# Dense products of the relational passes: h in a 12-bit part and the rest, two float32r products per block in place of one float32

## The chip, the cores and the metric

The kernel runs on one core of a Trainium2 chip, in one launch. The metric is the device time of one execution in microseconds; the executions of the kernel before took 5861.25 to 5871.9 us, with a median of 5869.68. The engines are named as in the profile: PE (matmul), PEld (its weight loads), DVE (vector), ACT (scalar), POOL (gathers), SP (most of the other DMAs).

## The reference

A graph network over 3125 nodes of 256 numbers and 100000 edges with a source, a target and one of 4 relations. The targets are the same in all layers; the shapes are fixed, the edges are data.

```python
# first pass: one graph convolution with a residual and a layernorm
h = x @ W                                     # (3125,256)@(256,256)
norm = deg_inv_sqrt[src] * deg_inv_sqrt[dst]
out = segment_sum(h[src] * norm[:, None], dst)
x = layernorm(x + out)
# four relational layers
inv_deg = 1 / max(cnt[dst, etype], 1)
for l in range(4):
    h = einsum('ni,rio->rno', X, W[l])        # 4 products (3125,256)@(256,256)
    agg = segment_sum(h[etype, src] * inv_deg[:, None], dst)
    out = agg + X @ root[l] + bias[l]
    X = elu(layernorm(out) * gamma[l] + beta[l]) + X
out = layernorm(x + X)
```

## The kernel before

The nodes are cut into `NW` = 25 windows of 128. All work is done in five **passes** (q = 0 for the first convolution, 1 to 4 for the relational layers). A pass takes h, which the pass before has stored in DRAM (`h_table`), and adds up for each window of targets what its edges bring. The edges are counted and sorted once, before pass 0. They come in two kinds.

**Gathered edges.** They are sorted by target window and cut into `NT` = 588 tiles of 128 edges. For a tile POOL gathers 128 rows of h (L584, an indirect DMA) into one of `RING` = 20 slots (16 in `msg`, 4 in `hout`); DVE makes the one-hot matrix `emat` of its targets and weights, 8 tiles ahead (L1409; ACT does it in pass 0); PE multiplies them (L758, float32, two instructions of 256 columns each) into one of `NPS` = 4 PSUM banks; DVE adds the bank to the window's sum (L1429). A slot and a bank are free again when PE and DVE say so.

**Dense edges.** The `K` = 7 chunks (128 source nodes each) with the most edges are kept in SBUF for a whole pass: SP loads them at the start of a pass, 7 pieces of 512 KB (L467). Their edges, `NDE` = 28000, were counted before pass 0 into blocks of 128 x 128 counts, one per source chunk, target window and relation. Each window of each pass multiplies its 28 blocks with the cached rows of h (`dense_product`, L736, float32), 700 products in a pass, and DVE adds the four sums with their weights (L1571). SP fetches the blocks of the next window as soon as PE has used those of the present one (L512, 7 pieces of 256 KB).

**Order of the work.** On PE the products of the tiles stand in a fixed order, and everything else is put before a tile by a table (`put(work, tile, step)`): window j ends at tile `done_at[j]`, and its dense products and its own window work are set by these two rules (DVE's table `steps` is of the same kind):

```python
done_at = [(j + 1) * NT // NW for j in range(NW)]
def dense_tile(j, i):
    d = done_at[j - 1] if j else 0
    return d + 1 + i * 16 // (K * R) if j else 14 + i * 7 // (K * R)
```

The window work is the transposes of the new X (L682), the four products with the next layer's weights (L690, 512 columns) and with its root (L700, L703), then DVE's layernorm and elu, ACT's copies, and the storing of h (SP, L503). The next pass begins when all h is stored. PE waits for a tile's gather (`s_msg`), its one-hot (`s_em`), a free bank (`s_acc`), and ahead of a dense product for the cached chunks (`s_hc`), the counts (`s_counts`) and the sums of the window before (`s_dense`).

**Before pass 0** (the first 1400 us) DVE counts the edges of every source chunk, chooses the 7 (L1124 to L1138), and the edges are sorted into tiles; then the count blocks are built from `DT` = 318 tiles of dense edges (L807, L811, L840) and stored in DRAM.

## Time and profile before

| | |
|---|---|
| median of 3 executions | 5869.68 us |
| span of the profiled execution | 5905.4 us |
| PE busy | 4806.4 us, 81% |
| PE weight loads | 3355.2 us, 57% |
| DVE busy | 3711.0 us, 63% |
| POOL busy | 3267.9 us, 55% |
| ACT busy | 1418.0 us, 24% |
| before pass 0 | 0 to 1400 us |
| pass 0, 1, 2, 3, 4 begin at | 1405, 2296, 3201, 4103, 5004 us |

The profiled execution's own time is its span, 5905.4 us; it is 35.7 us longer than the median. The busy shares are means over stages that differ: the stages before pass 0 have little POOL work, and in the passes PE, DVE and POOL pass each tile on. A long busy time says nothing by itself; the idle times before instructions, with the engine that ended them, say who waits.

### The profile page before, as it was taken

How to read it: one execution, taken by the hardware profiler on the slowest of the kernel's cores; microseconds unless marked ns; L12 is line 12 of the kernel's file. 1: busy time of each engine (PE TensorE's matmuls, PEld its weight loads, DVE VectorE, ACT ScalarE, POOL GpSimd, SP SyncE). 2: the span in 40 equal slices, each digit the busy share in tenths (PEclk: the TensorE clock that was granted, in tenths of full speed). 3: DMA queues.
4: the chain of work that ended last, by engine and by line, in shares of the span. 5: the costliest groups of instructions: out<-in, count | busy, mean ns of one | idle time of the engine just before them, and what ended most of it. 6: DMA issues, size and time to landing. Idle time of an engine off the chain costs nothing.

```text
span 5905.4 us, 80081 instructions
## 1 busy us (share of the span) xinstructions
PE 4806.4 (81%) x20415; PEld 3355.2 (57%) x20415; DVE 3711.0 (63%) x9969; ACT 1418.0 (24%) x3629; POOL 3267.9 (55%) x3256
## 2 busy tenths in 40 slices
PE   5878876777888887888887888887888888777776
PEld 4544432345666665666664666665666665556555
DVE  7998885565666664555554555555556555566665
ACT  1046653213555551111111111111111111011011
POOL 0058871003666664666664666665666664666664
PEclk8999998999999998999998999998999998888888
DMA  1000016312555555555555555555555555444444
GB/s 49 1 1 1 1 21 228 143 61 89 159 156 161 162 158 170 161 157 155 159 157 150 162 156 159 159 155 161 155 158 155 159 159 152 144 143 145 143 140 126
DMA packets 398886, 772.61 MB, mean 131 GB/s; under 512 B 77327, under 2 KB 166113, under 8 KB 398424
## 3 DMA queue, kind: packets, MB, share of 16 engines
q0 software_dynamic: 150720, 386.19, 24.2%
q1 hardware_dynamic: 246824, 380.53, 19.2%
q8 instruction: 162, 2.65, 0.2%
q10 hardware_dynamic: 1008, 1.84, 0.1%
q14 instruction: 172, 1.41, 0.1%
HBM read 652.04 MB, written 115.89 MB: 130 GB/s over the span
## 4 chain that ended last, share of the span: by engine, by line
PE 65%; issue 13%; DVE 12%; another core or an unknown queue 5%; ACT 2%; DVEq 2%; DMA 1%; ACTq 0%; SPq 0%
PE psum L736 24%; PE psum L758 23%; PE psum L690 5%; PE psum L807 3%; DVE arena L1429 3%; PE psum L840 2%; PE psum L793 2%; DVE arena L1571 2%; DVE arena L1303 2%; DVE arena L1290 2%; PE psum L700 1%; DVE arena L1238 1%; PE psum L622 1%; DVE emat L1409 1%
## 5 line engine op out<-in xcount | busy, mean ns | idle before, releaser
L584 POOL DMA_INDIRECT msg<-h_table,g_rel x1880 | 1795.6, 955 | 1088.5 <-issue 419.9
L1429 DVE TENSOR_TENSOR arena<-arena,psum 128x256 f32 x2940 | 1224.7, 417 | 1434.8 <-PE psum L758 970.4
L758 PE MATMUL psum<-msg,emat 128*128 128x256 f32 x4704 | 1519.7, 413 | 547.7 <-issue 323.1
L758 PEld LDWEIGHTS psum<-msg,emat 128*128 128x128 f32 x4704 | 892.9, 202 | 1021.7 <-issue 795.6
L1409 DVE TENSOR_SCALAR emat<-iota,node,weight 128x128 f32<-128x128 f32 x2352 | 862.9, 368 | 139.4 <-issue 58.8
L736 PE MATMUL psum<-arena,emat 128*128 128x256 f32 x3200 | 908.1, 405 | 6.3 <-issue 6.1
L584 POOL DMA_INDIRECT msg<-h_table,g_src x472 | 457.0, 968 | 726.3 <-PE psum L758 591.0
L736 PEld LDWEIGHTS psum<-arena,emat 128*128 128x128 f32 x3200 | 647.5, 204 | 134.0 <-issue 35.5
L566 POOL DMA_INDIRECT placed_rows<-leaving,idx x300 | 439.6, 1465 | 423.3 <-issue 416.7
L584 POOL DMA_INDIRECT hout<-h_table,g_rel x472 | 451.3, 956 | 275.4 <-issue 110.2
L793 PE MATMUL psum<-arena,emat 125*128 125x453 f16 x2000 | 448.0, 358 | 85.9 <-DVE arena L1303 85.9
L1376 DVE SCALAR_TENSOR_TENSOR found<-iota,key,arena 128x512 f16<-128x512 f32 x588 | 440.6, 749 | 87.3 <-issue 35.5
L758 PE MATMUL psum<-hout,emat 128*128 128x256 f32 x1176 | 377.9, 411 | 141.5 <-issue 82.5
L690 PE MATMUL psum<-w_sb,xt 128*128 128x512 f32 x800 | 445.8, 647 | 18.4 <-issue 16.3
L736 PE MATMUL psum<-arena,more_blocks 128*128 128x256 f32 x1600 | 425.6, 379 | 0.0
L758 PEld LDWEIGHTS psum<-hout,emat 128*128 128x128 f32 x1176 | 220.7, 200 | 259.4 <-issue 210.7
L1028 ACT ACTIVATE emat<-emat,arena 125x128 f16<-125x128 f16 x1000 | 302.9, 387 | 214.1 <-DVE emat L1282 214.1
L736 PEld LDWEIGHTS psum<-arena,more_blocks 128*128 128x128 f32 x1600 | 304.9, 191 | 41.8
L793 PEld LDWEIGHTS psum<-arena,emat 125*128 125x128 f16 x2000 | 163.4, 98 | 261.0 <-DVE arena L1303 145.7
L999 ACT ACTIVATE emat<-hout,ones 128x128 f32<-128x128 f32 x588 | 210.2, 395 | 392.0 <-PE psum L758 296.0
L736 PE MATMUL psum<-hout,more_blocks 128*128 128x256 f32 x1000 | 277.1, 381 | 0.0
L909 ACT COPY hout<-psum 128x512 f32<-128x512 f32 x200 | 114.0, 582 | 645.1 <-remote 314.1
(253 smaller groups left out, 5331.1 us busy)
## 6 DMA issues: line engine op xcount, KB each, us to landing
emat<-count_blocks SPq DMA_DIRECT2D x496, 256.0 KB
more_blocks<-count_blocks SPq DMA_DIRECT2D x372, 256.0 KB
count_blocks<-emat SPq DMA_DIRECT2D x200, 256.0 KB
h_table<-hout SPq DMA_DIRECT2D x100, 512.0 KB
msg<-h_table,g_rel POOLq DMA_INDIRECT x1880
arena<-h_table SPq DMA_DIRECT2D x24, 512.0 KB
msg<-h_table,g_src POOLq DMA_INDIRECT x472
hout<-h_table,g_rel POOLq DMA_INDIRECT x472
```

Source lines behind the costliest of these rows:

```text
L566: pool.indirect_dma_start(out=placed_dram[:, :], out_offset=bass.IndirectOffsetOnAxis(ap=idx[0:EP, n:n + 1], axis=0), in_=leaving[:, n, :] ...
L584: pool.indirect_dma_start(out=slots[n % RING], out_offset=None, in_=table[:, :], in_offset=bass.IndirectOffsetOnAxis(ap=rows[:, t:t + 1], ...
L690: mm = pe.matmul(win_ps[h][:, :], xt[:, 0, k * P:(k + 1) * P], w_sb[:, k, 2 * h:2 * h + 2, :].rearrange("p r o -> p (r o)"), start=(k == 0 ...
L736: mm = pe.matmul(to, blocks[c][:, r * P:(r + 1) * P], rows, start=(c == 0 and first), stop=(c == K - 1 and last))
L758: pe.matmul(agg_ps[n % NPS][:, 0:D], emat[:, n % BODY, :], slots[n % RING], start=True, stop=True).then_inc(s_mm, 1)
L793: pe.matmul(ps[half][:, 0:HB], slot[:, n, :], tile_hot[:, n, half * HB:(half + 1) * HB], start=False, stop=False)
L807: return pe.matmul(cols(psum, at, R * P), zeros16[:, 0:P], zeros16[:, :], start=True, stop=False)
L999: act.activation(emat[:, t % BODY, :], square[:, i * P:(i + 1) * P], ACT.Relu, bias=ones[:, 0:1], scale=-1.0).then_inc(s_em, 1)
L1028: a = act.activation(slot[:, n, :], lane_hot[:, b, m, :], ACT.Copy, scale=val[:, bass.ds(i * SU + k, 1)])
L1376: return dve.scalar_tensor_tensor(found[:, :, :], key_v, key[:, t:t + 1], inv_v[:, :, bass.ds(w, 1), :].rearrange("p r w d -> p r (w d)"), ...
L1409: dve.tensor_scalar(emat[:, n % BODY, :], iota[:, 0:P], node[:, t:t + 1], weight[:, t:t + 1], ALU.is_equal, ALU.mult).then_inc(s_em, 1)
L1429: dve.tensor_tensor(a, a, agg_ps[n % NPS][:, 0:D], ALU.add).then_inc(s_acc, 1)
```

## The change

1. `dense_product`: in passes 1 to 4 each block is multiplied twice, as float32r, with the two parts of h in the new tile `cache` (K x R x 2 x 256 float32r). Pass 0 keeps its one float32 product.
2. The parts: SP loads a chunk into part 1; DVE masks off the low 12 bits into a scratch tile (`cache_mask`), ACT copies it as float32r into part 0 (`high_parts`), DVE subtracts part 0 from part 1 (`cache_rest`). These steps stand among DVE's steps 3 to 16 of each relational pass. PE waits for each chunk (`s_split`) in the first window.
3. A chunk takes at most `MOST` = 4096 edges. The choice of chunks is written anew with this cap. `NDE` goes from 28000 to 26321, `NT` from 588 to 600, `DT` from 318 to 304.
4. Slot and relation of a dense edge are put in its sort key, and its decoding is written for that.
5. SBUF: the new cache takes the place of what only the stages before pass 1 need; the blocks have a tile of their own (`counts`); the x of the last residual is no longer loaded whole at the start of pass 1, but 128 KB per window in the last pass (`fetch_x1`).

```diff
-    NDE = E * K // NW
+    MOST = 1 << 12
+    NDE = min(MOST * f + (K - f) * (E - MOST * f) // NW for f in range(K + 1))
...
+        cache = sb("cache", [P, K, R, 2, D], f32r)
...
+                        sp.dma_start(cache[:, i, :, 1, :].bitcast(f32),
+                                     h_views[q % 2][bass.ds(c, 1), :, :, :]
+                                     .rearrange("w p r o -> (w p) r o")).then_inc(s_hc[i], 16)
...
-                if q == 1:
-
+                if q == L:
                     sp.wait_ge(s_x1w, (NW + ONE0) * 16)
-                    sp.dma_start(X1.rearrange("p (w d) -> p w d", w=NW),
-                                 x1_dram.rearrange("(w p) d -> p w d", p=P)).then_inc(s_x1, 16)
 
                 def store(j):
...
+                def fetch_x1(j):
+                    v = window_at(mybir.EngineType.SP, j)
+                    if j >= 2:
+                        sp.wait_ge(s_fin, (j - 2) * NFIN + 2)
+                    sp.dma_start(x1_slots[j % 2], x1_view[bass.ds(v, 1), :, :]
+                                 .rearrange("w p d -> (w p) d")).then_inc(s_x1[j % 2], 16)
...
             def dense_product(q, j, i):
                 n, (c, r) = q * NW + j, divmod(i, R)
                 if i == 0:
-                    pe.wait_ge(s_hc, (q + 1) * (16 * K))
+                    if q == 0:
+                        pe.wait_ge(s_first_cache, 16 * K)
                     if n:
                         pe.wait_ge(s_dense, n)
                 if r == 0:
                     pe.wait_ge(s_counts[c], (n + 1) * 16)
+                    if q and j == 0:
+                        pe.wait_ge(s_split, (q - 1) * K + c + 1)
                 if q:
-                    to, first = dense_ps[r // 2][:, r % 2 * D:(r % 2 + 1) * D], r % 2 == 0
-                    last = r % 2 == 1
-                    rows = hcaches[c][:, r, :]
+                    for part in range(2):
+                        mm = pe.matmul(dense_ps[r // 2][:, r % 2 * D:(r % 2 + 1) * D],
+                                       blocks[c][:, r * P:(r + 1) * P], cache[:, c, r, part, :],
+                                       start=(c == 0 and r % 2 == 0 and part == 0),
+                                       stop=(c == K - 1 and r % 2 == 1 and part == 1))
                 else:
-                    to, first, rows = dense_ps[0][:, 0:D], r == 0, hcache0[c]
-                    last = r == R - 1
-                mm = pe.matmul(to, blocks[c][:, r * P:(r + 1) * P], rows,
-                               start=(c == 0 and first), stop=(c == K - 1 and last))
+                    mm = pe.matmul(dense_ps[0][:, 0:D], raw_blocks[c][:, r * P:(r + 1) * P],
+                                   hcache0[c], start=(c == 0 and r == 0),
+                                   stop=(c == K - 1 and r == R - 1))
                 if r == R - 1:
...
+            def high_parts(q):
+                for c in range(K):
+                    act.wait_ge(s_masked, (q - 1) * K + c + 1)
+                    act.copy(cache[:, c, :, 0, :], masked).then_inc(s_high, 1)
...
-            done(dve.scalar_tensor_tensor(size_key[:, :], misc_ps[:, 256:256 + NW], 32.0,
-                                          iota[:, 0:NW], ALU.mult, ALU.add))
-            done(dve.tensor_tensor(pair_a, over_windows(size_key[:, :]),
-                                   by_window(size_key[:, :]), ALU.is_gt))
-            done(dve.tensor_reduce(place[:, :], pair_a, AXX, ALU.add))
-            done(dve.tensor_tensor(pair_a, over_windows(place[:, :]), by_window(iota[:, 0:NW]),
-                                   ALU.is_equal))
-            done(dve.tensor_tensor(pair_b, pair_a, over_windows(iota[:, 0:NW]), ALU.mult))
-            done(dve.tensor_reduce(top[:, :], pair_b, AXX, ALU.add))
+            for i in range(K):
+                done(dve.scalar_tensor_tensor(place[:, :], taken[:, :], float(-MOST),
+                                              misc_ps[:, 256:256 + NW], ALU.mult, ALU.add))
+                done(dve.tensor_scalar(place[:, :], place[:, :], 0.0, float(MOST),
+                                       ALU.max, ALU.min))
+                done(dve.scalar_tensor_tensor(size_key[:, :], place[:, :], 32.0, iota[:, 0:NW],
+                                              ALU.mult, ALU.add))
+                done(dve.tensor_reduce(best[:, :], size_key[:, :], AXX, ALU.max))
+                dve.scalar_tensor_tensor(chosen[:, :], size_key[:, :], best[:, :], iota[:, 0:NW],
+                                         ALU.is_equal, ALU.mult, accum_out=top[:, K - 1 - i:K - i])
+                done(dve.scalar_tensor_tensor(order[:, :], size_key[:, :], best[:, :],
+                                              taken[:, :], ALU.is_equal, ALU.mult,
+                                              accum_out=part_of[:, K - 1 - i:K - i]))
+                done(dve.scalar_tensor_tensor(taken[:, :], size_key[:, :], best[:, :],
+                                              taken[:, :], ALU.is_equal, ALU.add))
             done(dve.tensor_copy(top_i[:, :], top[0:1, 0:K]))
+            for i in range(K):
+                done(dve.tensor_scalar(hits[2], s_hi, top[0:EP, i:i + 1], 0.0,
+                                       ALU.is_equal, ALU.add, accum_out=row_n[0:EP, i:i + 1]))
+            dve.sem_inc(s_tot, 1)
+            dve.wait_ge(s_base, 2)
+            dve.tensor_copy(row_first[0:EP, :], misc_ps[0:EP, 0:K])
+            done(dve.tensor_scalar(top_rank[0:EP, :], part_of[0:EP, :], float(MOST), float(MOST),
+                                   ALU.mult, ALU.add))
             for i in range(K):
                 done(dve.tensor_scalar(hits[2], s_hi, top[0:EP, i:i + 1], float(i + 1),
                                        ALU.is_equal, ALU.mult))
-                done(dve.tensor_tensor(d_place, d_place, hits[2], ALU.add))
+                done(dve.tensor_scalar(hits[1], hits[2], 1.0, None, ALU.min))
+                done(dve.tensor_tensor_scan(runs[2], one_row, hits[1], row_first[0:EP, i:i + 1],
+                                            ALU.mult, ALU.add))
+                done(dve.scalar_tensor_tensor(hits[2], runs[2], top_rank[0:EP, i:i + 1], hits[2],
+                                              ALU.is_le, ALU.mult))
+                done(dve.tensor_tensor(d_place, d_place, hits[2], ALU.max))
             done(dve.tensor_scalar(hits[2], d_place, 0.0, None, ALU.is_gt, ALU.add,
...
-            split_values(a_d, b_d, c_d, e_d)
+            done(dve.tensor_scalar(c_d, a_d, 2, P - 1, ALU.arith_shift_right, ALU.bitwise_and))
+            done(dve.tensor_scalar(e_d, b_d, 10, None, ALU.arith_shift_right))
+            dve.scalar_tensor_tensor(d_slot[:, :], e_d, float(P), c_d, ALU.mult, ALU.add)
+            done(dve.tensor_scalar(b_d, b_d, 3, P - 1, ALU.arith_shift_right, ALU.bitwise_and))
+            done(dve.tensor_scalar(a_d, a_d, R - 1, None, ALU.bitwise_and))
             done(dve.scalar_tensor_tensor(d_key[:, :], a_d, float(P), b_d, ALU.mult, ALU.add))
-            done(dve.tensor_scalar(e_d, c_d, P - 1, None, ALU.bitwise_and))
-            done(dve.tensor_copy(d_slot[:, :], e_d))
-            done(dve.tensor_scalar(c_d, c_d, 7, None, ALU.arith_shift_right))
-            chunk, part = e_d.bitcast(f32), a_d.bitcast(f32)
-            done(dve.tensor_copy(chunk, c_d))
-            for i in range(K):
-                if i % KH:
-                    done(dve.tensor_scalar(part, chunk, top[:, i:i + 1], float(i % KH * P),
-                                           ALU.is_equal, ALU.mult))
-                    done(dve.tensor_tensor(d_slot[:, :], d_slot[:, :], part, ALU.add))
...
+            def cache_mask(q, c):
+                dve.wait_ge(s_hc[c], q * 16)
+                dve.wait_ge(s_high, (q - 1) * K + c)
+                dve.tensor_scalar(masked.bitcast(i32), cache[:, c, :, 1, :].bitcast(i32),
+                                  HI_MASK, None, ALU.bitwise_and).then_inc(s_masked, 1)
+
+            def cache_rest(q, c):
+                dve.wait_ge(s_high, (q - 1) * K + c + 1)
+                dve.tensor_tensor(cache[:, c, :, 1, :], cache[:, c, :, 1, :].bitcast(f32),
+                                  cache[:, c, :, 0, :].bitcast(f32), ALU.subtract
+                                  ).then_inc(s_split, 1)
...
+                if q:
+                    for c in range(K):
+                        steps[SPLIT0 + c * SPLITS] = lambda c=c: cache_mask(q, c)
+                        steps[SPLIT0 + 1 + c * SPLITS] = lambda c=c: cache_rest(q, c)
+                assert SPLIT0 + K * SPLITS <= done_at[0] - DA
```

PE, the first dense products of pass 1 (window 0). A row's count is of matmul calls; a float32 call of 128x256 is two instructions in the trace. The program names a tile by its place in memory, so the cached rows and count blocks read as `hout` and `emat` before. Before:

```order
L758 MATMUL psum<-msg,emat 128x256 x14
L736 MATMUL psum<-hout,emat 128x256 x4
L758 MATMUL psum<-msg,emat 128x256
L736 MATMUL psum<-hout,emat 128x256 x4
L758 MATMUL psum<-msg,emat 128x256
L736 MATMUL psum<-hout,emat 128x256 x4
```

and now:

```order
L803 MATMUL psum<-msg,emat 128x256 x14
L775 MATMUL psum<-cache,counts 128x256 x8
L803 MATMUL psum<-msg,emat 128x256
L775 MATMUL psum<-cache,counts 128x256 x8
L803 MATMUL psum<-msg,emat 128x256
L775 MATMUL psum<-cache,counts 128x256 x8
```

The dense products stand ahead of the same tiles, and each call of float32 has become two of float32r.

PE again, the last dense products of a window in the same pass, where the next layer's products (L690, now L731) begin. Before:

```order
L682 MATMUL psum<-ident,hout 128x128 x2
L736 MATMUL psum<-w_sb,more_blocks 128x256 x2
L758 MATMUL psum<-msg,emat 128x256
L736 MATMUL psum<-w_sb,more_blocks 128x256
L758 MATMUL psum<-msg,emat 128x256
L736 MATMUL psum<-w_sb,more_blocks 128x256 x2
L758 MATMUL psum<-hout,emat 128x256
L736 MATMUL psum<-w_sb,more_blocks 128x256
L736 MATMUL psum<-hout,more_blocks 128x256
L758 MATMUL psum<-hout,emat 128x256
L690 MATMUL psum<-w_sb,xt 128x512
L736 MATMUL psum<-hout,more_blocks 128x256 x2
```

and now:

```order
L803 MATMUL psum<-hout,emat 128x256
L775 MATMUL psum<-cache,counts 128x256 x4
L803 MATMUL psum<-hout,emat 128x256
L723 MATMUL psum<-ident,hout 128x128 x2
L775 MATMUL psum<-cache,counts 128x256 x4
L803 MATMUL psum<-hout,emat 128x256
L775 MATMUL psum<-cache,counts 128x256 x2
L803 MATMUL psum<-msg,emat 128x256 x3
L731 MATMUL psum<-w_sb,xt 128x512
```

The spread over 16 tiles is as it was (two products ahead of most tiles, one ahead of some), with twice the calls; the layer products follow it a few tiles later.

DVE, the start of pass 1: one-hots (L1409, now L1479) and adds (L1429, now L1499; a row ISA is its wait). Before:

```order
L1409 TENSOR_SCALAR emat<-iota,node,weight 128x128 x8
L1416 TENSOR_LOAD win_i
L1409 TENSOR_SCALAR emat<-iota,node,weight 128x128
L1429 ISA
L1429 TENSOR_TENSOR arena<-arena,psum 128x256
L1409 TENSOR_SCALAR emat<-iota,node,weight 128x128
L1429 ISA
L1429 TENSOR_TENSOR arena<-arena,psum 128x256
L1409 TENSOR_SCALAR emat<-iota,node,weight 128x128
L1429 ISA
```

and now:

```order
L1499 ISA
L1499 TENSOR_TENSOR acc<-acc,psum 128x256
L1479 TENSOR_SCALAR emat<-iota,node,weight 128x128
L1499 ISA
L1499 TENSOR_TENSOR acc<-acc,psum 128x256
L1650 TENSOR_SCALAR hout<-cache 128x1024
L1479 TENSOR_SCALAR emat<-iota,node,weight 128x128
L1499 ISA
L1499 TENSOR_TENSOR acc<-acc,psum 128x256
L1655 TENSOR_TENSOR cache<-cache 128x4x256
L1479 TENSOR_SCALAR emat<-iota,node,weight 128x128
```

From the third add on, a mask (L1650) or a subtraction (L1655) stands between an add and the next one-hot, 14 of them in 14 steps.

## Rows read from the trace of the kernel before

**Rows 1.** Busy time by stage; columns: stretch, length, engines, clock, DMA share, GB/s.

```profile
0.00:330.00 330.00, 241.26 (x1217) 159.68 (x1217) 284.83 (x533) 19.03 (x51) 4.90 (x15) 0.92 0.08 22
...
900.00:1400.00 500.00, 359.99 (x1890) 183.08 (x1888) 280.83 (x980) 105.23 (x196) 18.67 (x20) 0.93 0.32 121
1400.00:2296.00 896.00, 764.68 (x2976) 562.14 (x2976) 568.63 (x1571) 450.00 (x1351) 552.12 (x568) 0.95 0.52 155
2296.00:3200.00 904.00, 764.36 (x2976) 566.21 (x2976) 510.05 (x1476) 138.40 (x225) 561.84 (x588) 0.95 0.53 160
...
4110.00:5004.00 894.00, 760.64 (x2974) 566.31 (x2974) 511.87 (x1475) 139.33 (x225) 555.96 (x583) 0.95 0.53 157
5004.00:5905.00 901.00, 681.18 (x2576) 518.50 (x2576) 537.62 (x1593) 89.30 (x125) 561.69 (x588) 0.87 0.49 143
```

**Rows 2.** The same for 100 us of pass 3 and of pass 4.

```profile
4300.00:4400.00 100.00, 85.48 (x349) 64.19 (x349) 58.10 (x169) 16.11 (x26) 64.72 (x69) 0.99 0.53 160
5200.00:5300.00 100.00, 79.52 (x310) 60.45 (x310) 62.23 (x190) 10.71 (x15) 65.39 (x69) 0.89 0.49 145
```

**Rows 3.** The page's part 4, the chain that ended last.

```profile
PE 65%; issue 13%; DVE 12%; another core or an unknown queue 5%; ACT 2%; DVEq 2%; DMA 1%; ACTq 0%; SPq 0%
PE psum L736 24%; PE psum L758 23%; PE psum L690 5%; PE psum L807 3%; DVE arena L1429 3%; PE psum L840 2%; PE psum L793 2%; DVE arena L1571 2%; DVE arena L1303 2%; DVE arena L1290 2%; PE psum L700 1%; DVE arena L1238 1%; PE psum L622 1%; DVE emat L1409 1%
```

**Rows 4.** Sums of waits: who waited for whom, us, times, longest.

```profile
POOL msg L584 <- PE psum L758: 978.4, 512, 481.9
DVE arena L1429 <- PE psum L758: 970.4, 618, 14.9
```

**Rows 5.** Timeline, PE, pass 4; columns: start, length, instruction, idle before.

```profile
5407.86 1.03 PE L736 MATMUL psum<-arena,emat 128*128 128x256 f32 x4
...
5412.61 1.03 PE L736 MATMUL psum<-arena,emat 128*128 128x256 f32 x4
5414.76 0.67 PE L758 MATMUL psum<-hout,emat 128*128 128x256 f32 x2 [1.12 <-issue]
```

**Rows 6.** Timeline, DVE, at the same place.

```profile
5414.19 0.42 DVE L1429 TENSOR_TENSOR arena<-arena,psum 128x256 f32 x1 [5.21 <-PE psum L758]
```

**Rows 7.** Timeline, POOL, in pass 1.

```profile
2601.05 0.94 POOL L584 DMA_INDIRECT hout<-h_table,g_rel  x1 [0.30 <-issue]
...
2606.65 0.94 POOL L584 DMA_INDIRECT hout<-h_table,g_rel  x1 [2.16 <-PE psum L758]
```

**Rows 8.** Timeline, PE, in pass 1.

```profile
3019.58 1.03 PE L736 MATMUL psum<-arena,emat 128*128 128x256 f32 x4
3020.44 0.59 PE L758 MATMUL psum<-msg,emat 128*128 128x256 f32 x2
```

**Rows 9.** Timeline, PE, while the count blocks are built (float16).

```profile
1100.00 0.60 PE L840 MATMUL psum<-emat 128*128 128x512 f16 x2
1100.43 0.17 PE L811 MATMUL psum<-zeros 128*128 128x1 f16 x1
```

**Rows 10.** The page's part 5: weight loads in float32 and in float16.

```profile
L736 PEld LDWEIGHTS psum<-arena,emat 128*128 128x128 f32 x3200 | 647.5, 204 | 134.0 <-issue 35.5
...
L793 PEld LDWEIGHTS psum<-arena,emat 125*128 125x128 f16 x2000 | 163.4, 98 | 261.0 <-DVE arena L1303 145.7
```

**Rows 11.** Timeline, DVE, choice of the chunks.

```profile
45.07 0.18 DVE L1124 SCALAR_TENSOR_TENSOR size_key<-psum,iota 128x25 f32<-128x25 f32 x1
...
49.70 0.43 DVE L1135 TENSOR_SCALAR arena<-arena,top 125x800 f16<-125x800 f16 x1
50.16 0.58 DVE L1137 TENSOR_TENSOR arena<-arena 125x800 f16<-125x800 f16 x1
...
57.22 0.99 DVE L1138 TENSOR_SCALAR_CACHE_REDUCE arena<-arena 125x800 f16<-125x800 f16 x1
...
60.99 1.88 DVE L1147 TENSOR_TENSOR_SCAN arena<-arena,d_first 125x800 f32<-125x800 f32 x1
```

**Rows 12.** Timeline, DVE, start of pass 1.

```profile
2322.19 0.42 DVE L1429 TENSOR_TENSOR arena<-arena,psum 128x256 f32 x1 [3.95 <-remote]
```

117 lines of the change are left out of this document (76 added, 41 removed).

## The prediction

> **What bounds the kernel now.** I read first the busy times by stage, to see whether the 81% of PE is an average over unlike stages. It is not quite. In each pass over the edges PE is busy 764 of about 904 us, DVE 510, POOL 562, and POOL issues 588 gathers, one per tile [rows 1]. Preparation before the first pass takes 1400 us. The last pass is the most telling row: it has 400 matmuls fewer, PE is busy 681 us instead of 761, and it still takes 901 us where the pass before took 894. The slices of 100 us say the same: 69 gathers in a slice of pass 3, with 85.5 us of PE, and 69 in a slice of pass 4, with 79.5 us of PE [rows 2]. That is a pace of 100 / 69 = 1.45 us per tile. A reader is to see here that PE time taken out of a pass need not come back as span.
>
> Then the chain of waits: 24% of the span runs through the dense product (L736), 23% through the tile product (L758), 12% through DVE and 13% is "issue", an engine waiting for nothing that shows [rows 3]. The sums of waits name the loop: DVE's add waits 970 us for the tile product, POOL's gather 978 us for the same line (a slot of the ring comes free when the tile is multiplied) [rows 4]. The timeline shows how. One stretch of PE, from 5407.86 on, is without a gap four rows of L758 (a tile each) and five of L736 with 18 instructions in all; the four tiles fill the four PSUM banks; DVE's first add comes only at 5414.19, after 5.21 us of idling, and PE starts again at 5414.76 after 1.12 us idle [rows 5, 6]. So a round of the loop is the stream of four tiles plus about 1.1 us.
>
> The third limit is POOL. A gather is 0.94 us and the next follows after 0.30, that is one per 1.25 us; a stall on the ring costs 2.16 instead of 0.30 [rows 7]. 1.25 us is the floor of a tile whatever PE does.
>
> **The dense products (the main term).** One block now costs two instructions of float32, started 0.216 us apart: 3019.58 to 3020.44 is four of them, 0.86 us [rows 8]. So a block is 0.433 us, and 700 of them in a pass are 303 us. After the change a block is also two instructions, each one float32r product of 256 columns. The trace has no float32r. The nearest row with a 2-byte type is the float16 product of 512 columns: two of them are passed in 0.43 us (1100.00 to 1100.43), 0.216 each, so 0.108 for 256 columns [rows 9]. Bounds: below, 0.108 an instruction, 0.216 a block; above, float32r as float32, two instructions of 0.216 for each of the two products, 0.866 a block. Between them stands the weight load: 204 ns mean for these float32 blocks, 98 ns for float16 [rows 10]; each block's weights are loaded twice, as now. At 0.2 us a load a block would cost 0.4 and nothing is won. I take 0.108 an instruction because both instructions and weights of one pass are near it in the float16 rows. That takes 0.217 x 700 = 152 us of PE work from each of passes 1 to 4, 608 in all; pass 0 keeps float32.
> The Trainium skill bears on this from both sides. "FP8 and Floating Point Precision", section TensorE Precision Notes, has true float32 as four passes and a reduced float32 that is read and cut to about 22 bits; a block in two single passes would be half of four, as the sum has it. "TensorE: Matmul & The Clock Gate", section on weight-path modes, gives the fast weight load to 128 weights of a type that is not FP32; if float32r counts as FP32 there, the weights stay at the 0.2 of the row, and the sum loses its main term. That is the fourth case below.
>
> **What of it reaches the end.** The order puts the dense products between tiles, 16 tiles of a window of 23.5; on average 28 x 2 / 16 = 3.5 instructions a tile. A round of four such tiles is (8 + 14) x 0.216 + 1.1 = 5.85 us, 1.46 a tile, which is the measured pace. After: 8 x 0.216 + 14 x 0.108 + 1.1 = 4.34 us, 1.09 a tile, below the 1.25 of POOL. So in these stretches the gather becomes the bound, but not cleanly: the ring is full, the sign of "done" comes in clumps of four, and each clump that comes late makes one gap of 2 us in POOL. The 7.5 tiles of a window without dense work keep their transposes and layer products. I take the mean of the present pace and the floor, weighted to the floor: 1.33 us per tile. Over the some 560 tiles of a pass that run at the pace now, that is 560 x 0.13 = -73 us a pass.
>
> **The tiles.** At most 4096 edges of a cached chunk become counts, which makes the dense part smaller: 26321 edges instead of 28000. NT goes from 588 to 600, so 12 gathers, products, one-hots and adds more in each of five passes. In passes 1 to 4, 12 x 1.33 = +16; in pass 0, 12 x 1.46 = +17.5. The building of the count blocks has 304 tiles instead of 318; that stage is at most 500 / 318 = 1.57 us a tile [rows 1]; 14 x 1.3 = -18.
>
> **The splitting.** In each pass from 1 on DVE masks and subtracts 7 chunks of 128x1024 and ACT copies them. DVE has nothing like it; the scan of 800 columns and the 800-column operation of 0.99 us [rows 11] bracket it at 0.7 to 1.3 us each, so about 13.5 us of DVE per pass and 7 of ACT. At the start of a pass DVE waits some 4 us before each add (3.95 before the one at 2322.19) [rows 12], and the split's steps, 3 to 16, lie just there; the order below the diff shows mask and subtraction between the adds. PE needs chunk c at tile 14 + c. The cover is these waits; without it the price is 13.5 us, and with a copy that DVE waits for, 20. Bounds 0 and +20 a pass; I take +5. DVE's in-order queue is the risk: the mask waits for a load of 512 KB, and the adds and one-hots behind it wait too.
>
> **Preparation.** The choice of the chunks is seven rounds of seven small operations at about 0.2 each (one over 25 columns took 0.18), 10 us, for the six operations that now stand from 45.07 to 49.5; seven counts at 0.99 and the reading of the sum, 8 us; and per chunk five operations of 800 columns with a scan of 1.88 instead of two (0.43 and 0.58 [rows 11]): 4.5 instead of 1.1, 24 us. With three more operations some +41; the shorter decoding gives 4.5 back. DVE is on the path there (285 of 330 us busy). Bounds +15 and +45. Net of preparation: 41 - 4.5 - 18 = +18.5.
>
> **Hidden edits.** x1 is no longer loaded as one 3.2 MB piece at the start of pass 1 but 128 KB a window in the last pass; DMA is at 0.53 and 0.49 of its time [rows 1], so I cost it at 0, with -8 to +10 as bounds. Loads of the cache are waited for one by one: 0, since the weights and blocks come as late.
>
> **Sum.** Passes 1 to 4: (-73 + 16 + 5) x 4 = -208. Pass 0: +17.5. Preparation: +18.5. Together -172 us on a span of 5905.4, so 5733. The median of the runs is 5869.7, 35.7 below that execution; the same distance gives 5698, say 5700. About 12 us (0.2%) is what a measurement here can tell from no change.
>
> **Rivals.**
> 1. Forecast: pace 1.33. For it: the round worked out above gives the pace now. Against: pass 4. 5700; its own range 5600 to 5810. Chance 0.39.
> 2. The floor: every tile at 1.25, as POOL's rows between stalls. 560 x 0.21 = -118, + 15 + 5, x 4 = -392, and +36: 5514. For it: 1.09 is well below 1.25. Against: POOL stalls at present though PE has gaps. Chance 0.21.
> 3. The other side: the pace stays 1.46. Pass 4 lost 80 us of PE work and gained nothing, so the loop PE - DVE - POOL may have its own period (DVE sees the four products late, POOL sees its slots late). Part of it can be the clock: it was granted 0.87 in pass 4 against 0.95 before [rows 1], and a less busy PE would again lose in clock what it gains in work. Then the price decides: 12 x 1.46 x 5 = 88, split 20, preparation 18.5: +126, 5996. It decides once the pace stays above 1.42. Chance 0.33. The skill's clock page ("TensorE: Matmul & The Clock Gate", HAM oscillation) has the same effect: PE that micro-idles between groups is throttled again and again; the 0.87 agrees in direction.
> 4. The change doesn't do what it says: float32r instructions are bound by 0.2 us weight loads (then as 3, about 6000) or run as float32, 0.433 more a block, x 2800 = +1212, about 7200. For it: the weight row of 204 ns. Chance 0.07, most of it at 6000.
>
> **From these the numbers.** Faster: 0.39 + 0.21, and a little of 3 where the pace falls to 1.40: 0.62. Same: between 1.40 and 1.42, 0.03. Slower: 0.35. The range 5490 to 6010 leaves out a floor that is undercut and float32r as float32. Since both signs have weight, the likeliest's own range stands above.
>
> **What the next profile would show.** Right: L775 at about 0.11 us between starts, with weight loads near 0.1; passes 1 to 3 near 850 us with 600 gathers, 73 to 75 gathers in a slice of 100 us; "POOL msg <- PE" much smaller. DVE's mask and subtraction within the first 60 us of a pass and no new wait before them; first stage longer by 40 us. Wrong if: weight loads of 0.2 set L775's starts (4), or 68 to 69 gathers a slice with PE more idle and a clock below 0.9 (3), or 79 to 80 gathers a slice (2).

## The result, and the profile after

The changed kernel took 5979.48 us (median of 4 runs, 5971.05 to 5985.01) against 5867.16 before on the same chip: ratio 1.0193, 95% interval 1.018 to 1.0205, 112 us slower. The profiled execution has a span of 5969.3 us.

Chips differ. The kernel before takes 5867 to 5913 us on some and 5235 to 5237 on two others (below: chips of the slower and of the faster kind), so every comparison of times here is between kernels on one chip. The profile of before that the prediction read has a span of 5905.4 us and is like the chip on which before took 5912.55 us in later runs; the profile below is from a chip on which gathers come 1.457 us apart in pass 1 instead of 1.475.

Busy time by stage of the changed kernel (columns as in [rows 1]): count blocks, pass 0, pass 1, pass 3 and pass 4.

```profile
940.00:1434.00 494.00, 351.16 (x1821) 178.22 (x1822) 273.74 (x953) 111.77 (x217) 19.52 (x21) 0.92 0.35 130
1434.00:2338.00 904.00, 763.07 (x2996) 566.44 (x2995) 586.35 (x1606) 454.98 (x1359) 559.51 (x580) 0.95 0.51 154
2338.00:3248.00 910.00, 698.05 (x3000) 523.76 (x3000) 532.09 (x1514) 145.42 (x231) 575.64 (x600) 0.87 0.52 157
...
4157.00:5065.00 908.00, 693.81 (x3000) 516.33 (x3000) 531.94 (x1515) 147.12 (x232) 577.46 (x600) 0.89 0.53 158
5065.00:5969.00 904.00, 612.25 (x2600) 487.62 (x2600) 556.91 (x1630) 97.91 (x133) 577.32 (x600) 0.78 0.50 148
```

Each pass takes 904 to 910 us, somewhat more than the 894 to 904 of [rows 1], though PE is busy some 66 us less (698 and 764 in pass 1), and 69 us less in pass 4. The granted clock went from 0.95 to 0.87 and 0.89 in passes 1 and 3, and from 0.87 to 0.78 in pass 4. Slices of 100 us, against [rows 2]:

```profile
4300.00:4400.00 100.00, 78.21 (x347) 58.13 (x346) 58.66 (x169) 15.30 (x26) 65.83 (x69) 0.91 0.51 156
5200.00:5300.00 100.00, 70.81 (x291) 56.71 (x292) 64.44 (x193) 9.14 (x13) 66.27 (x70) 0.74 0.50 149
```

69 gathers there before, 69 now; 69 in the last pass before, 70 now, with 70.8 us of PE instead of 79.5. The page's chain of waits, against [rows 3]: the dense product has gone from 24% to 16% (L775 with 11% in passes 1 to 4, L780 with 5% in pass 0), and "issue" (13% to 16%) and the tile product (L803, 23% to 26%) have taken its place.

```profile
PE 61%; issue 16%; DVE 13%; another core or an unknown queue 3%; ACT 2%; DVEq 2%; DMA 1%; SPq 0%; POOL 0%; ACTq 0%
PE psum L803 26%; PE psum L775 11%; PE psum L731 5%; PE psum L780 5%; DVE acc L1499 4%; PE psum L838 3%; PE psum L852 3%; PE psum L885 2%; DVE acc L1641 2%; DVE arena L1379 2%; DVE arena L1366 2%; PE psum L741 1%; DVE emat L1479 1%; PE psum L656 1%
```

The sums of waits, against [rows 4]: POOL and DVE still wait for the product of the tile.

```profile
POOL msg L618 <- PE psum L803: 846.1, 434, 468.7
DVE acc L1499 <- PE psum L803: 781.4, 554, 14.4
```

How one tile's product is passed on is seen on PE (start, length, instruction, idle before), with DVE and POOL below. The sign of a product is the semaphore update by which PE tells DVE and POOL that it is done.

```profile
3002.76 0.82 PE L775 MATMUL psum<-cache,counts 128*128 128x256 f32 x4
3003.43 0.67 PE L803 MATMUL psum<-msg,emat 128*128 128x256 f32 x2
...
3004.41 0.67 PE L803 MATMUL psum<-msg,emat 128*128 128x256 f32 x2
...
3010.46 0.67 PE L803 MATMUL psum<-msg,emat 128*128 128x256 f32 x2 [2.42 <-issue]
```

```profile
3009.89 0.42 DVE L1499 TENSOR_TENSOR acc<-acc,psum 128x256 f32 x1 [2.56 <-remote]
```

```profile
3503.79 0.94 POOL L618 DMA_INDIRECT hout<-h_table,g_rel  x1 [0.30 <-issue]
3505.04 0.95 POOL L618 DMA_INDIRECT hout<-h_table,g_rel  x1 [0.30 <-issue]
3507.75 0.94 POOL L618 DMA_INDIRECT hout<-h_table,g_rel  x1 [1.76 <-remote]
```

Three things are to be seen. The tile product that starts at 3004.41 ends in the record at 3005.08; DVE adds it at 3009.89, 4.8 us later, and had been idle for 2.56 us before. PE, with all four banks full, starts again at 3010.46 after 2.42 us idle, more than the 1.12 of [rows 5]. POOL keeps its 1.25 us between stalls of 1.76 where it waits for a slot.

The four float32r instructions from 3002.76 to 3003.43 seem to take 0.67 us, against 0.86 for four of float32 [rows 8], but this reading misleads: the first of them starts in the record too soon after the float32 product ahead of it. From one tile product to the next is the safe measure. In the run with half the gathers (below), where PE hardly waits, it is 0.90 us with two blocks between:

```profile
3200.39 0.59 PE L805 MATMUL psum<-msg,emat 128*128 128x256 f32 x2
3200.63 0.82 PE L777 MATMUL psum<-cache,counts 128*128 128x256 f32 x4
3201.28 0.60 PE L805 MATMUL psum<-msg,emat 128*128 128x256 f32 x2
```

The median of 427 such stretches in passes 1 and 2 is 0.900 us, and 1.295 (of 436) in its partner with float32 products; with one block between it is 0.671 and 0.863. So the second block adds 0.23 us in float32r and 0.43 in float32: an instruction of float32r takes 0.115 us, whether the weights change before it or not.

The weight load of a block did not get shorter as the float16 one is:

```profile
L775 PE MATMUL psum<-cache,counts 128*128 128x256 f32 x5600 | 1355.3, 363 | 41.6 <-issue 41.4
L775 PEld LDWEIGHTS psum<-cache,counts 128*128 128x128 f32 x5600 | 1002.4, 215 | 182.6 <-issue 75.9
```

Its mean record is 215 ns, while the products with these weights start 0.115 us apart: the loads overlap, and their length does not set the pace.

The split, at the start of pass 1 (mask, copy on ACT, subtraction, next mask):

```profile
2349.17 0.69 DVE L1650 TENSOR_SCALAR hout<-cache 128x1024 int32<-128x1024 int32 x1
...
2350.97 1.27 DVE L1655 TENSOR_TENSOR cache<-cache 128x1024 fp32r<-128x1024 f32 x1 [0.53 <-issue]
...
2352.75 0.68 DVE L1650 TENSOR_SCALAR hout<-cache 128x1024 int32<-128x1024 int32 x1
```

```profile
2349.89 1.05 ACT L997 CAST cache<-hout 128x1024 fp32r<-128x1024 f32 x1 [13.62 <-DVE hout L1650]
```

A chunk takes 3.6 us in the chain mask 0.69, copy 1.05, subtraction 1.27, between the adds. PE's idle time before L775 is 41.6 us in all four passes, 41.4 of it put down to "issue" and not to DVE. The choice of chunks (first small operation, first count, first scan, last STT of the seven):

```profile
44.75 0.18 DVE L1177 SCALAR_TENSOR_TENSOR place<-taken,psum 128x25 f32<-128x25 f32 x1
...
56.16 1.05 DVE L1193 TENSOR_SCALAR_CACHE_REDUCE arena<-arena,top 125x800 f16<-125x800 f16 x1
...
65.64 1.88 DVE L1204 TENSOR_TENSOR_SCAN arena<-arena,row_first 125x800 f32<-125x800 f32 x1
...
94.46 1.05 DVE L1206 SCALAR_TENSOR_TENSOR arena<-arena,top_rank 125x800 f16<-125x800 f32 x1
```

It ends at some 96.1 us; in the kernel before the last of these adds ended at 57.2 ([rows 11]). That is 39 us longer; 41 were forecast. POOL's first 20 gathers, which fill the ring long before pass 0, begin at 939.9 us instead of 899.8, 40 us later.

### The profile page after: what moved, and what is told of

Its sections match the earlier page's. It is cut to its first block, busy times and chain, and to the rows that moved or that the text cites. A ratio compares the mean times of both kernels' runs of the same rounds, so it can differ in the third digit from the quotient of the medians.

```text
span 5969.3 us, 80103 instructions
## 1 busy us (share of the span) xinstructions
PE 4519.0 (76%) x20453; PEld 3180.7 (53%) x20453; DVE 3830.7 (64%) x10216; ACT 1458.2 (24%) x3681; POOL 3334.8 (56%) x3316
## 3 DMA queue, kind: packets, MB, share of 16 engines
q14 instruction: 177, 1.45, 0.1%
## 4 chain that ended last, share of the span: by engine, by line
PE 61%; issue 16%; DVE 13%; another core or an unknown queue 3%; ACT 2%; DVEq 2%; DMA 1%; SPq 0%; POOL 0%; ACTq 0%
PE psum L803 26%; PE psum L775 11%; PE psum L731 5%; PE psum L780 5%; DVE acc L1499 4%; PE psum L838 3%; PE psum L852 3%; PE psum L885 2%; DVE acc L1641 2%; DVE arena L1379 2%; DVE arena L1366 2%; PE psum L741 1%; DVE emat L1479 1%; PE psum L656 1%
## 5 line engine op out<-in xcount | busy, mean ns | idle before, releaser
L803 PE MATMUL psum<-msg,emat 128*128 128x256 f32 x4800 | 1664.4, 442 | 742.8 <-issue 456.1
L1499 DVE TENSOR_TENSOR acc<-acc,psum 128x256 f32 x3000 | 1250.2, 417 | 1418.5 <-PE psum L803 781.4
L803 PEld LDWEIGHTS psum<-msg,emat 128*128 128x128 f32 x4800 | 893.1, 216 | 1166.4 <-issue 1003.5
L775 PE MATMUL psum<-cache,counts 128*128 128x256 f32 x5600 | 1355.3, 363 | 41.6 <-issue 41.4
L775 PEld LDWEIGHTS psum<-cache,counts 128*128 128x128 f32 x5600 | 1002.4, 215 | 182.6 <-issue 75.9
L1479 DVE TENSOR_SCALAR emat<-iota,node,weight 128x128 f32<-128x128 f32 x2400 | 876.6, 366 | 138.9 <-issue 80.6
L803 PE MATMUL psum<-hout,emat 128*128 128x256 f32 x1200 | 422.9, 443 | 194.2 <-issue 116.0
L838 PE MATMUL psum<-arena,build 125*128 125x452 f16 x2000 | 445.6, 356 | 87.6 <-DVE arena L1379 87.6
L731 PE MATMUL psum<-w_sb,xt 128*128 128x512 f32 x800 | 462.0, 668 | 6.5 <-issue 4.7
L803 PEld LDWEIGHTS psum<-hout,emat 128*128 128x128 f32 x1200 | 220.9, 215 | 290.4 <-issue 248.3
L1079 ACT ACTIVATE build<-build,arena 125x128 f16<-125x128 f16 x1000 | 302.9, 388 | 213.6 <-DVE build L1358 213.6
L838 PEld LDWEIGHTS psum<-arena,build 125*128 125x128 f16 x2000 | 162.7, 97 | 261.8 <-DVE arena L1379 147.0
L780 PE MATMUL psum<-hout,counts 128*128 128x256 f32 x1000 | 267.0, 382 | 2.9 <-issue 2.9
L1641 DVE SCALAR_TENSOR_TENSOR acc<-psum,inv,acc 128x256 f32 x400 | 193.6, 484 | 82.1 <-issue 34.7
L780 PEld LDWEIGHTS psum<-hout,counts 128*128 128x128 f32 x1000 | 191.8, 192 | 49.8 <-issue 25.7
```

The lines of the kernel that those rows point to most:

```text
L731: mm = pe.matmul(win_ps[h][:, :], xt[:, 0, k * P:(k + 1) * P], w_sb[:, k, 2 * h:2 * h + 2, :].rearrange("p r o -> p (r o)"), start=(k == 0 ...
L775: mm = pe.matmul(dense_ps[r // 2][:, r % 2 * D:(r % 2 + 1) * D], blocks[c][:, r * P:(r + 1) * P], cache[:, c, r, part, :], start=(c == 0 a ...
L780: mm = pe.matmul(dense_ps[0][:, 0:D], raw_blocks[c][:, r * P:(r + 1) * P], hcache0[c], start=(c == 0 and r == 0), stop=(c == K - 1 and r = ...
L803: pe.matmul(agg_ps[n % NPS][:, 0:D], emat[:, n % BODY, :], slots[n % RING], start=True, stop=True).then_inc(s_mm, 1)
L838: pe.matmul(ps[half][:, 0:HB], slot[:, n, :], tile_hot[:, n, half * HB:(half + 1) * HB], start=False, stop=False)
L1079: a = act.activation(slot[:, n, :], lane_hot[:, b, m, :], ACT.Copy, scale=val[:, bass.ds(i * SU + k, 1)])
```

## The experiments

In the edits, `...` marks lines left out.

### The changed kernel again, and where the loss comes from

> The changed kernel as it is, beside the kernel before on one chip. Where the signs of finished products come late (4 us, as in the traces of the prediction), pace 1.46 per tile and 1.9% slower than before. Where they come at once (0.15 us), the gather's 1.25 us sets the pace of both kernels, and this is slower by the 12 tiles of five passes (12 x 1.26 x 5 = 76 us), the longer choice (27 to 40 us) less 0 to 10: ratio 1.018 to 1.023 there too. Theory W (the float32r products bring something wherever PE is the bound) would have it faster than before on one of the two.

Measured: 6021.46 us against 5912.55, ratio 1.019 (1.0176 to 1.0204). Its spans by stage can be set beside the profile of before, since the chip is alike: pass 0 (its first gather after the 20 that fill the ring) begins 27 us later (40 up to the first gathers, 12.5 back in the count blocks), and the five passes take 17.8, 14.3, 15.4, 19.1 and 13.7 us more. 12 tiles at the measured 1.475 us are 17.7. So 27 + 80 = 107.7 us is the whole loss, and pass 0, which has no float32r and no split, loses as much as the others: float32r and the split leave no mark of more than a few us in a pass.

> The changed kernel as it is. Gather theory: where the kernel before takes 5235 us, pace 1.26 for both, 12 x 1.26 x 5 = 76 us for the tiles and 27 to 40 for the choice of chunks, 5340 to 5350 us, ratio 1.020 to 1.022, the same as with float32 products in its place (5350). Where it takes 5900: 1.019. Work theory: where signs come at once PE is 96% busy with float32 products, so float32r should win something there: below 5320.

Measured on another chip: 5980.4 against 5869.0, ratio 1.0199 (1.018 to 1.0217).

```diff
-    MOST = 1 << 12
-    NDE = min(MOST * f + (K - f) * (E - MOST * f) // NW for f in range(K + 1))
+    MOST = 1 << 17
+    NDE = E * K // NW
```

> The changed kernel without the cap of 4096 edges per chunk: 28000 dense edges, 588 gathered tiles and 318 dense tiles as before the change, all else changed (for other edges than these a count could be too large for 12 bits). If the loss is the 12 more tiles in five passes: 60 x 1.26 to 1.46 = 76 to 88 less, 18 to 20 more for 14 tiles of the count blocks, so 55 to 70 us below the changed kernel and 25 to 50 us above the one before: ratio 1.005 to 1.01. If the loss is the split or the waits for it: nothing of it comes back, ratio 1.02.

Measured: 5950.72 us against 5912.55, ratio 1.0063 (1.0048 to 1.0079); 71 us below the changed kernel on that chip. Two thirds of the loss come from the cap. With as many tiles as before, this is also the direct comparison of float32r with float32. Pass 1 of the kernel before, then of this one:

```profile
2296.00:3200.70 904.70, 764.36 (x2976) 566.21 (x2976) 510.32 (x1476) 138.75 (x225) 561.85 (x589) 0.95 0.53 160
2352.50:3254.90 902.40, 680.75 (x2976) 509.34 (x2976) 520.79 (x1490) 145.46 (x231) 566.98 (x589) 0.89 0.53 157
```

PE is busy 84 us less and the pass is 2 us shorter; passes 1 to 4 together take 3603.7 us instead of 3609.4. So the float32r products and the split, taken together, win or lose next to nothing where the gathers come 1.475 us apart.

What is left over is preparation: in the profiled executions pass 0 begins 52 us later than before. The choice of chunks is 38 of it. From the first gathers to the last product of the count blocks it is 508 us instead of 495, with 318 tiles in both; no run shows where these 13 us come from. With the 304 tiles of the changed kernel this stage takes 482 us here, and 479 to 486 in ten profiles. (The medians differ by 38 us and these two executions by 51: this one is the slowest of its four.)

### Float32 products in the changed kernel

```diff
-                    for part in range(2):
-                        mm = pe.matmul(dense_ps[r // 2][:, r % 2 * D:(r % 2 + 1) * D],
-                                       blocks[c][:, r * P:(r + 1) * P], cache[:, c, r, part, :],
...
+                    mm = pe.matmul(dense_ps[r // 2][:, r % 2 * D:(r % 2 + 1) * D],
+                                   raw_blocks[c][:, r * P:(r + 1) * P],
+                                   cache[:, c, r, 1, :].bitcast(f32),
```

It multiplies the rest part alone, in float32; the high part is left out.

> The changed kernel with the dense products of passes 1 to 4 as one float32 product again (of the unsplit h; the split is still made and not used). Theory L (latency): with gathers running, the sign that a tile's product is done reaches DVE about 4 us late, and four PSUM banks turn that into 5.85 us per four tiles; PE work between tiles costs nothing as long as it fits. Then this takes as long as the changed kernel, 5970 to 6010 us, with 68 to 69 gathers in 100 us. Theory W (work): the streams of PE set the pace and the float32r products did bring something that other parts ate: then the 150 us of PE work a pass show, 6100 or more.

Measured: 5350.12 us (before 5234.77, ratio 1.022, 1.0203 to 1.0237), on a chip of the faster kind, for which the expectation had no figure; on late signs it says nothing. There the kernel with float32r (and six banks in the last pass, below) took 5351.06 us in its one run: no difference. 600 us of a pass with float32 products, and then with float32r:

```profile
3100.00:3700.00 600.00, 574.39 (x2394) 437.69 (x2393) 428.96 (x1197) 111.73 (x180) 454.44 (x478) 1.00 0.61 184
```

```profile
3100.00:3700.00 600.00, 506.82 (x2389) 379.00 (x2389) 420.08 (x1193) 111.64 (x179) 454.65 (x478) 0.97 0.61 183
```

478 gathers in both, 1.255 us each, which is the floor of [rows 7]. PE is busy 574 us in the one (96%) and 507 in the other; the 68 us stay unused.

### Half the gathers: what a float32r product is worth

```diff
                 for t in range(NT):
                     n = q * NT + t
+                    if q and t % 2:
+                        continue
...
-                    pe.wait_ge(s_msg[n % RING], (n // RING + 1) * 16)
+                    pe.wait_ge(s_msg[n % RING], (NT // RING if q and t % 2 else n // RING + 1) * 16)
```

Odd slots keep the rows of pass 0; their gathers in passes 1 to 4 are left out.

> The changed kernel with every second gather of passes 1 to 4 left out (its slot keeps old rows), all other work as it was. Theory L with a sign that is late by itself, whatever the traffic: pace 1.46, total within 50 us of the changed kernel. Theory G (what makes the sign late is the gathering: its DMAs or POOL's work): the signs come earlier and the pace falls towards 1.0, what the end of a pass without gathers shows: some 4 x 560 x 0.4 = 900 us less, about 5050.

Measured: 4641.05 us, 602 to 603 us in each of passes 1 to 3, but on a chip of the faster kind, where it can't tell L from G. A repeat on the second chip of the faster kind:

> The changed kernel with every second gather of passes 1 to 4 left out, again, beside the float32 one of 731 us per pass. Where gathers are not the bound, float32r is worth what PE saves: 602 us a pass where signs come at once; theory G (half the gathers, no late signs) gives 600 to 615 here too, so 120 to 130 us a pass below float32; theory L (signs late by themselves) gives 800 or more.

Measured: 4641.56 us. With float32 products (of the rest part), on a chip where the signs come late:

> Every second gather of passes 1 to 4 left out, with the dense products as one float32 each (of the rest part): the partner of the run with half the gathers and float32r (602 us per pass where signs come at once, 0.94 per tile). Where the gather no longer bounds, PE does, and the float32r products show what they are worth: 700 x 0.433 against 700 x 0.34 as its trace has it between starts, about 60 to 70 us a pass, so 660 to 670 us a pass; if the block in float32r really cost 0.216 it would be 150, 750 us a pass.

Measured: 5274.55 us, 731 us a pass. Since this and the float32r run were on different chips, both were run on one:

> Every second gather of passes 1 to 4 left out, float32 products (of the rest part). PE-bound at 0.433 a block: 725 to 735 us a pass, whichever the chip.

> The same with the float32r products, on the same chip: 600 to 605 us a pass where signs come at once (measured so), the same or up to 640 where they come late. The difference to the float32 one, divided by 700 blocks, is what a block in float32r saves: 125 us would be 0.18 of 0.433.

Measured on that chip: 5264.32 us with float32, 4777.46 with float32r. Pass 2 with float32, then pass 2 with float32r:

```profile
3075.00:3808.00 733.00, 712.73 (x3000) 564.57 (x3000) 543.22 (x1515) 147.32 (x232) 286.37 (x301) 0.98 0.47 142
```

```profile
2948.00:3550.00 602.00, 579.00 (x3000) 461.18 (x3000) 518.49 (x1514) 147.57 (x232) 295.31 (x300) 0.98 0.57 173
```

In both PE is busy 96 to 97% of the pass. The pass is 732 us with float32 and 603 with float32r: 129 us, or 0.184 per block, so that a block is worth 0.433 - 0.184 = 0.249 us where PE is the bound; the starts above give 0.23. The forecast had 0.216 and 152 us. The expectation for the first pair (60 to 70 us, from 0.34 a block) rested on the misleading 0.67 us for four and was too low. The price of the product was about right. What failed is that it was paid where nobody waited.

This pair, on a chip of the slower kind, also says something of the 1.46 us. POOL still waits for the tile 20 before, as in the changed kernel, so a ring whose round takes a fixed 20 x 1.46 = 29 us would hold the tiles at 1.46 us here too. They come every 603 / 600 = 1.0 us. So the pace of 1.46 depends on the gathers, and it is not a fixed round of the ring.

### Three banks, six banks: is it a round of the banks?

```diff
-    NPS = 4
+    NPS = 3
```

> The changed kernel with three PSUM banks for the tiles instead of four. Theory L: one bank's round (product 0.5, late sign 4.1, add 0.42, start again) is about 5.8 us whatever the number of banks, so the pace in the body of a pass becomes 5.8 / 3 = 1.93 us per tile instead of 1.46: some +0.47 x 560 x 5 = +1300 us, 7200 to 7350. Theory W or theory G (the gathers and their ring set the pace): the pace stays near 1.46, less than +200 us.

> The changed kernel with three PSUM banks for the tiles, again, since the first time the signs of products came at once (0.15 us) and its pace was the gather's. Where the signs come 4 us late: theory L (one bank's round is 5.8 us) gives 1.93 us per tile, +0.46 x 2900 = +1300 us over the changed kernel; theory G (the pace belongs to the gathers: whatever delays the signs lets one tile pass in 1.47 us) gives 1.47 to 1.6, less than +350 us. Where they come at once: 5350 to 5370 as before.

Measured: 5358.16 and 5365.72 us on the two chips of the faster kind, pace 1.265, 7 and 10 us more than the next kernel below on the same chips, in one run each. On such a chip a sign comes at once, so these two runs say nothing on theory L (a bank's round of some 5.8 us sets the pace). PE and DVE of the run with six banks:

```profile
3304.19 1.05 PE L809 MATMUL psum<-msg,emat 128*128 128x256 f32 x2
3304.69 1.17 PE L780 MATMUL psum<-cache,counts 128*128 128x256 f32 x4
```

```profile
3305.39 0.42 DVE L1505 TENSOR_TENSOR acc<-acc,psum 128x256 f32 x1 [0.48 <-PE psum L809]
```

The product's record ends at 3305.24 and DVE adds at 3305.39. Over the tiles before whose add DVE had idled for more than 0.3 us, the median from the end of the product's record to the add is 0.15 us there and 4.1 us in the changed kernel's first profile (766 and 805 tiles).

> The changed kernel with three PSUM banks for the tiles. Where signs come late, theory L (one bank's round is 5.8 us, the banks share it): 1.93 us per tile, +1300 us over the changed kernel, 7200 or more. Theory G (the pace is the gathers' own, late signs are its symptom): 1.47 to 1.6, 5980 to 6350. Where signs come at once: 5355 to 5370, and the question stays open.

Measured where the signs come late: 5975.36 us (before 5867.35), the same as the next kernel below on this chip (5975.44), which has four banks in passes 0 to 3. 700 us of a pass with four banks (on a chip like it, where the changed kernel took 5980) and with three:

```profile
3350.00:4050.00 700.00, 535.28 (x2392) 405.97 (x2390) 414.88 (x1197) 111.49 (x180) 457.47 (x479) 0.91 0.52 158
```

```profile
3350.00:4050.00 700.00, 540.21 (x2406) 406.80 (x2405) 419.20 (x1203) 112.62 (x181) 459.47 (x481) 0.91 0.53 158
```

479 and 481 gathers, 1.46 us each. Theory L, which had 1.93, is refuted: taking one bank away costs nothing.

```diff
+        last_ps = banks[0:4] + banks[6:8]
+        def agg_bank(n):
+            return last_ps[n % 6] if n >= L * NT else agg_ps[n % NPS]
```

> The changed kernel with six PSUM banks for the tiles in the last pass alone, where the banks of the next layer's products are free. Theory L: the last pass is then bound by the gather, 1.25 us per tile instead of 1.45, so 100 to 115 us shorter, 5860 to 5880 in all, and more than 75 gathers in 100 us there. Theory G: the ring or the gathers' traffic delays the signs, and more banks only make them later: no change, 5970 to 5990.

> The changed kernel with six PSUM banks in the last pass, again, for the same reason. Where signs are late: theory L, last pass 100 us shorter than the others, 1.25 to 1.3 per tile; theory G, 1.46 as in the others. Where they come at once: no change.

> The changed kernel with six PSUM banks in the last pass. Where signs come late, theory L: the last pass is 100 us or more shorter than the passes before it; theory G: within 10 us of them (905). Where signs come at once: 5350 to 5356.

Measured: 5351.06 and 5355.38 us where signs come at once, 5975.44 where they come late. Pass 3 with four banks and pass 4 with six there:

```profile
4159.00:5067.00 908.00, 679.15 (x3000) 503.70 (x3000) 532.67 (x1515) 147.50 (x232) 578.02 (x600) 0.90 0.53 158
5067.00:5973.00 906.00, 636.03 (x2600) 485.75 (x2600) 553.34 (x1630) 98.01 (x133) 576.00 (x600) 0.78 0.50 148
```

908 and 907 us: nothing won. The signs were later instead. In the last pass the median from the end of the record to the add, over the tiles for which DVE had idled for more than 0.3 us, is 3.3 us with three banks, 4.6 with four (the changed kernel's profile) and 7.3 with six (159, 155 and 140 tiles), at one pace of 1.45 us. So the lateness of a sign follows the number of banks, and the pace does not: a late sign is not what sets it.

### Without refills of the count blocks

```diff
-                refill(0, 1)
+                if q == 0:
+                    refill(0, 1)
...
-                    pe.wait_ge(s_counts[c], (n + 1) * 16)
+                    pe.wait_ge(s_counts[c], (min(n, NW) + 1) * 16)
```

Passes 1 to 4 use the blocks of the first window all through; their refills are left out.

> The changed kernel without the refills of the count blocks in passes 1 to 4 (7 DMAs of 256 KB a window; the blocks stay those of the first window). If the late signs come from the number of bytes or of DMAs in flight, the pace falls in proportion to the DMAs that are gone (7 of 31 a window, a third of the bytes): 1.25 to 1.35 instead of 1.47, 300 to 500 us less. If they come from the gathers alone (POOL's writing of descriptors), less than 60 us change. Where signs come at once: no change.

Measured: 5333.27 us on a chip where signs come at once, 22 us below the run with six banks there.

```profile
3100.00:3700.00 600.00, 511.67 (x2397) 378.31 (x2396) 424.45 (x1198) 111.49 (x179) 454.32 (x479) 0.98 0.42 123
```

479 gathers in 600 us, with a DMA share of 0.42 instead of 0.61: with a third less for the DMA engines to do, the floor of the gather stays. That goes with POOL's own rows, 0.95 us busy and 0.30 to the next. What it would do where signs come late was not measured.

### Fewer gathers

```diff
-    K = 7
+    K = 8
```

> The changed kernel with 8 cached chunks instead of 7 (NDE 29762, 574 gathered tiles, 332 dense tiles; key, found and the first pass's seventh and eighth chunk lie in other places of SBUF, the split begins two steps earlier). If the number of gathers sets the time: 26 x 5 x 1.26 = 164 us below the changed kernel (1.46: 190), 28 dense tiles more cost 42, one round more in the choice 5 and in the split 0 to 8: 110 to 145 us below it and 0 to 30 us below the kernel before, ratio 0.993 to 1.0. If PE sets it, 400 more float32r instructions of passes 1 to 4 and 100 float32 products in pass 0 cost more than the gathers bring: ratio above 1.01.

Measured: 5907.3 us against 5912.55, ratio 0.9991 (0.9982 to 1.0). That is 114 us below the changed kernel on the same chip, as reckoned from the gathers, at a pace of 1.48 (110 to 145 were expected).

The last one is float32 throughout: `cache` holds h in one part, with no mask, copy or subtraction, the choice of chunks is the one before the change, `NDE = E * K // NW`, and K is 8. Its first lines of difference to the changed kernel:

```diff
-    K = 7
+    K = 8
...
-        cache = sb("cache", [P, K, R, 2, D], f32r)
+        cache = sb("cache", [P, K, R, D])
```

> Float32 products as before the change, with 8 chunks in the cache (32000 dense edges, 556 gathered tiles, 350 dense tiles), the old choice of chunks without a cap, no split; x1 is fetched by window as in the changed kernel, which makes the room. Gather theory: against the kernel before 32 x 5 = 160 gathers less, at 1.26 us 200 us (at 1.47, 235), 32 dense tiles more 48: 5085 us where before takes 5235 (ratio 0.971), 5725 where it takes 5912 (0.968). Work theory: 100 float32 blocks more a pass are 43 us of PE: it eats what the gathers bring, ratio 0.99 to 1.0. Where signs come at once PE is then near the bound itself (about 1.22 of 1.26 us a tile), so 0.975 is as likely as 0.971.

Measured: 5727.74 us against 5869.0, ratio 0.9761 (0.974 to 0.9782), the best against the kernel before of all here that compute the whole result. The expectation had 0.968 for such a chip.

```profile
4100.00:4800.00 700.00, 638.97 (x2670) 493.46 (x2669) 414.64 (x1213) 117.92 (x191) 455.07 (x479) 1.00 0.56 171
```

PE is busy 91% of the time with more float32 products than ever, and the gathers still come at 700 / 479 = 1.46 us. Against the kernel before, 160 gathers less at 1.46 are 234 us, and its pass 0 begins 56 us later than in the profile of before (32 dense tiles more, for which 48 us had been expected): 178 were to be won, and 141 are. The rest is in the passes, beside the changed kernel on that chip: from the last gather of a pass to the first of the next it takes 43 to 46 us instead of 33 to 36, and the gathers come at 1.466 to 1.484 us in passes 1 to 3 instead of 1.454 to 1.458. That PE's work begins to show at 91% would fit this; no run separates it.

## Why the prediction was wrong

- **What bounds the kernel.** The rows on which it rested were right, and two of its observations were the answer: 69 gathers per 100 us in every pass, and pass 4, which lost 80 us of PE work and gained nothing. It gave the third rival, which says this, 0.33 and 5996 us; 5979 came out.
- **The dense products.** Sized at 0.216 us a block and 152 us a pass; 0.249 and 129 measured by the pair with half the gathers. Right in kind. The weight loads stayed at 215 ns in the records, and still did not bind as the fourth case had it: the products with them start 0.115 us apart.
- **What of it reaches the end. This is the step that failed.** "A round of four such tiles is (8 + 14) x 0.216 + 1.1 = 5.85 us, 1.46 a tile, which is the measured pace" is a coincidence of numbers. From it came a pace of 1.33 us and -73 us a pass. The pace stayed: with the same 588 tiles, the four passes took 3603.7 us instead of 3609.4. The 1.1 us in the sum was no fixed price; in the stretches shown PE idles 1.1 us after float32 and 2.4 after the shorter stream. Three, four and six banks have one pace, float32 with 8 chunks and float32r with 7 too. The pace goes with the gathers: 1.25 to 1.26 us on one kind of chip, 1.46 to 1.48 on the other.
- **The tiles.** 12 more per pass: +16 forecast, +14 to +19 measured. Pass 0: +17.5 against +17.8. Count blocks: -18 forecast for 14 tiles at 1.3 us, -12.5 measured. The tiles give more than that back (26 us from 508 to 482, 1.9 a tile; two other pairs of runs give 1.35 and 1.65), but at the same number of tiles the stage is 13 us longer, which the sum did not have.
- **The splitting.** +5 a pass forecast; float32r products and split together measured -6 us in four passes. Mask, copy and subtraction had 0.69 to 1.27 us as bounded, and lay in DVE's waits.
- **Preparation.** +41 against 39 for the choice; the 4.5 us back from the shorter decoding are not seen, since the first gathers are 40 us later. Net with the blocks 18.5 against 27.
- **The clock.** Between the kernel before and the one without the cap it fell from 0.95 to 0.89 in pass 1, as the third rival had it, while PE's idle time in the pass grew from 140 to 222 us. In the trace it stands at full (2.4 GHz) or at half (1.2 GHz) and nothing between; in pass 2 of the changed kernel, for instance, it falls at 3366.23 us, after PE had idled 2.18 us from 3363.64 on. Part of the saved work is taken back with it, as far as can be told: PE is 84 us less busy in that pass, against 134 between the two with half the gathers, both at 0.98. But on the faster kind of chip it was 0.97 in the slice above with float32r and 1.00 with float32, and the time was the same; and with half the gathers it was 0.98 on the slower kind too. So it is a consequence here: PE idles and is granted less, and still has 222 us to spare. The Trainium skill, "TensorE: Matmul & The Clock Gate", section HAM oscillation, has a PE that waits between its matmuls throttled again; the trace agrees in direction.

Open is why on some chips the gather takes 1.46 us and the sign of a finished product comes 4 us late. The two go together in all profiles. Half the gathers make most signs punctual in the float32 run there (median 0.15 us in passes 1 to 4), and more banks make them later; that would fit signs that are handed on at a limited rate which gathers use up. This is argued and not shown. The number of ring slots was not varied; the pair with half the gathers rules out a round of fixed length only.

## What to carry to other kernels

An engine that is 81% busy with 65% of the chain is not the bound when a pass with less of its work takes as long: count the slowest thing that goes with each step (here gathers per 100 us) in stages with different work, before pricing what the busy engine would save. A model of a round that hits the measured pace is no proof; change one of its numbers first (here three banks instead of four). And where the number of gathers sets the time, spend memory on fewer gathers: 8 cached chunks in plain float32 gave 2.4%, float32r products that cost 12 tiles a pass and a longer preparation lost 1.9%.
